# Decoder layer on one core: the gate projected together with the shared values, the shared keys by themselves, and the hand-written orders rewritten

## The reference

```
x = layernorm(x + attention(x))            # 16 query heads, 4 key/value heads of 128, rotary, softmax, Wo
x = layernorm(x + longconv(ctx, ctx, x))   # 16 heads of 8: kv = k_i v_j, causal convolution with ssm_kernel + D, times q_i
x = layernorm(x + gated(x))                # below
```

```
gating     = softmax(x @ W_gate.T)                     # 16 columns
indicator  = one_hot(argmax(gating)); top1 = max(gating)
q, k, v    = split(x @ W_qkv.T)                        # 16 heads of 16 each
k_shared   = sum over heads of indicator * k           # one key of 16 per token
v_shared   = sum over heads of indicator * top1 * v    # one value of 16 per token
att        = softmax(causal(q . k_shared / sqrt(16)))  # per head
y          = att @ v_shared
```

## Time and profile before

| | |
|---|---|
| runs | median 321.51 us of 3 (321.10 to 321.72) |
| profiled execution | 321.38 us, of it 319.6 us span |
| TensorE busy | 95% of the span |
| VectorE, ACT, GpSimd busy | 78%, 72%, 63% |
| chain that ended last | TensorE 72%, VectorE 14%, ACT 4%, GpSimd 2%, issue 6% |
| mean granted TensorE clock | 0.993 of 2.4 GHz |

### The profile page before, as it was taken

How to read it: one execution, slowest core, us unless ns; L and a number is a source line. 1 busy time by engine, 2 the same in 40 slices (tenths; PEclk the granted TensorE clock), 3 DMA queues, 4 the chain that set the end, 5 groups by cost and what they waited for, 6 DMA issues and landing times.

```text
span 319.6 us, 6276 instructions
## 1 busy us (share of the span) xinstructions
PE 305.0 (95%) x2073; PEld 242.0 (76%) x2073; DVE 250.6 (78%) x504; ACT 230.4 (72%) x695; POOL 201.2 (63%) x289
## 2 busy tenths in 40 slices
PE   6997999999999999999999999999999999999981
PEld 2896898889888889888878979877557666666550
DVE  3779868847976776776686898989999999986764
ACT  3889597869778777767875687733578877788780
POOL 0698885766754777656393278995986976720031
PEclk9999999999999999999999999999999999999997
DMA  5961103101010313213000000000000000000010
GB/s 179 295 281 49 53 3 98 30 6 67 2 33 2 114 37 104 78 37 108 0 3 0 2 1 1 2 0 3 0 3 0 18 1 3 16 3 18 17 35 33
DMA packets 6176, 13.87 MB, mean 43 GB/s; under 512 B 896, under 2 KB 3328, under 8 KB 5888
## 3 DMA queue, kind: packets, MB, share of 16 engines
q1 hardware_dynamic: 5872, 13.34, 12.7%
q10 hardware_dynamic: 272, 0.13, 0.1%
HBM read 12.42 MB, written 1.05 MB: 42 GB/s over the span
## 4 chain that ended last, share of the span: by engine, by line
PE 72%; DVE 14%; issue 6%; ACT 4%; DMA 2%; POOL 2%; SPq 0%; POOLq 0%; DVEq 0%; ACTq 0%
PE bank L415 16%; PE bank L563 14%; PE bank L452 8%; PE bank L437 7%; PE bank L524 4%; PE bank L674 3%; PE bank L632 3%; DVE t_cos L1811 3%; PE bank L685 2%; PE bank L547 2%; DMA w_raw<-in_wqkv 2%; PE bank L542 2%; DVE fneg_max L1868 2%; PE bank L544 2%; PE bank L669 1%
## 5 line engine op out<-in xcount | busy, mean ns | idle before, releaser
L2320 POOL TENSOR_TENSOR t_sin<-rot,sin 128x512 f32<-128x512 f32 x36 | 46.8, 1307 | 31.1 <-ACT rot L1151 25.4
L2348 POOL TENSOR_TENSOR prob<-prob,rden 128x512 f32<-128x512 f32 x32 | 37.2, 1164 | 33.9 <-DVE rden L1711 33.8
L1186 ACT ACTIVATE prob<-bank,neg_max 128x128 f32<-128x128 f32 x128 | 45.4, 377 | 2.3 <-DVE neg_max L1704 2.2
L563 PE MATMUL bank<-wo_hi,head_hi 128*128 128x256 f32 x128 | 40.2, 314 | 0.0
L1266 ACT ACTIVATE prob<-bank,fneg_max 128x128 f32<-128x128 f32 x128 | 36.6, 379 | 4.7 <-DVE fneg_max L1868 4.7
L415 PE MATMUL bank<-x_hi,w_hi 128*128 128x512 f32 x96 | 33.5, 429 | 3.4 <-DVE t_cos L1619 1.9
L563 PE MATMUL bank<-wo_lo,head_hi 128*128 128x256 f32 x128 | 36.0, 281 | 0.0
L563 PE MATMUL bank<-wo_hi,head_lo 128*128 128x256 f32 x128 | 35.9, 280 | 0.0
L1150 ACT COPY rot<-bank 64x512 f32<-64x512 f32 x40 | 23.4, 584 | 13.9 <-PE bank L415 12.5
L2310 POOL TENSOR_TENSOR kv<-ctxT 128x256 f32<-128x256 f32 (+3 forms) x64 | 31.8, 529 | 1.0 <-PE bank L437 1.0
L1619 DVE TENSOR_TENSOR t_cos<-bank,cos 128x512 f32<-128x512 f32 x36 | 24.6, 687 | 9.5 <-ACT rot L1151 9.0
(11 more groups left out here) (134 smaller groups left out, 807.3 us busy)
## 6 DMA issues: line engine op xcount, KB each, us to landing
w_raw<-in_wqkv SPq DMA_DIRECT2D x4, 768.0 KB, 4.4
toep<-in_toep SPq DMA_DIRECT2D x8, 256.0 KB, 2.8
wo_raw<-in_wo SPq DMA_DIRECT2D x4, 512.0 KB, 3.5
ctxT<-in_ctx SPq DMA_DIRECT2D x1, 1024.0 KB, 4.9
x<-in_x SPq DMA_DIRECT2D x1, 1024.0 KB, 9.6
out<-x SPq DMA_DIRECT2D x8, 128.0 KB, 1.7
wf<-in_wf SPq DMA_DIRECT2D x1, 784.0 KB, 4.7
x_raw<-in_xt SPq DMA_DIRECT2D x2, 256.0 KB, 4.5
```

Source lines behind the costliest of these rows:

```text
L563: last = pe.matmul(acc_bank[k // 2][:, (k % 2) * D:(k % 2 + 1) * D], hp[:, k % 2, h * P:(h + 1) * P], wp[:, g % 2, h, :], start=(h + n == ...
L1186: last = act.activation(prob[:, k % 2, h * P:(h + 1) * P], score_bank[k % 2][:, h * P:(h + 1) * P], ACT.Exp, bias=neg_max[:, k % 2, h:h + ...
L2320: pool.tensor_tensor(t_sin[:, par, :].rearrange("p (b t) -> p b t", b=BH), rot[:, par, :].rearrange("p (b t) -> p b t", b=BH), sin[:, :].u ...
L2348: pool.tensor_tensor(own, own, rden[:, k % 2, :].unsqueeze(2).to_broadcast([P, HG, P]), ALU.mult).then_inc(norm_done, 1)
```

## The change

The gate's 16 columns join the 256 of the shared values in one matmul of 272 columns (per c), into `kvf_bank`; the shared keys get a matmul of their own, 256 columns, into the upper half of `tf_bank`, beside the queries. The gate no longer waits for `kblock_done`, the keys do. `query_project` loses its wait for `gate_done`. The mask becomes two products, one from each bank, and waits for `qf_done`, the copy of the queries out of `tf_bank`. The lists of TensorE, ACT, VectorE and GpSimd are rewritten from the start to the end; SP's isn't. The functions:

```diff
-            def gate_project(b):
+            def value_project(b):
                 j = b % 2
                 pe.wait_ge(in_ffn, 48)
                 pe.wait_ge(x2copy_done, b + 1)
+                if b == 0:
+                    pe.wait_ge(acc_done, 2 * UNITS - 1)
+                at_least(pe, masked_done, b, 1)
+                at_least(pe, ynorm_done, b, 3)
+                for c in range(C):
+                    last = pe.matmul(kvf_bank[:, 0:D + FH], x2T[:, j, c * P:(c + 1) * P],
+                                     wf[:, c, 2 * D:3 * D + FH], start=(c == 0), stop=(c == C - 1))
+                last.then_inc(gate_mm_done, 1)
+
+            def key_project(b):
+                j = b % 2
                 at_least(pe, kblock_done, b, 1)
                 for c in range(C):
-                    last = pe.matmul(tf_bank[:, D:D + FH], x2T[:, j, c * P:(c + 1) * P],
-                                     wf[:, c, 3 * D:3 * D + FH], start=(c == 0), stop=(c == C - 1))
-                last.then_inc(gate_mm_done, 1)
...
+                    last = pe.matmul(tf_bank[:, D:2 * D], x2T[:, j, c * P:(c + 1) * P], wf[:, c, D:2 * D],
+                                     start=(c == 0), stop=(c == C - 1))
+                last.then_inc(kvf_done, 1)
 
             def query_project(b):
                 j = b % 2
-                pe.wait_ge(gate_done, b + 1)
...
-                act.mul(gate[:, :], tf_bank[:, D:D + FH], -1.0).then_inc(gate_done, 1)
+                act.mul(gate[:, :], kvf_bank[:, D:D + FH], -1.0).then_inc(gate_done, 1)
...
                 dve.wait_ge(kvf_done, b + 1)
-                dve.tensor_tensor(kv_masked[:, :, :, :],
-                                  kvf_bank[:, :].rearrange("p (n d h) -> p n d h", n=2, h=FH),
-                                  chosen[:, :].unsqueeze(1).unsqueeze(2).to_broadcast([P, 2, FD, FH]),
-                                  ALU.mult).then_inc(masked_done, 1)
+                dve.wait_ge(qf_done, b + 1)
+                for n, source in enumerate((tf_bank[:, D:2 * D], kvf_bank[:, 0:D])):
+                    last = dve.tensor_tensor(kv_masked[:, n, :, :], source.rearrange("p (d h) -> p d h", h=FH),
+                                             chosen[:, :].unsqueeze(1).to_broadcast([P, FD, FH]), ALU.mult)
+                last.then_inc(masked_done, 1)
```

The ramp, ACT and then VectorE:

```diff
             split_x(1)
+            split_wo(0)
             copy_v(0)
-            split_wo(0)
             exps(0, 0)
...
             exps(0, 2)
-            first_conv_copy()
             item(0, "Q1")
...
             split_x(1)
+            row_max(0, 0)
             value_low(0)
-            row_max(0, 0)
             row_max(0, 1)
...
+            cos_item(0, "K")
             row_max(0, 2)
-            cos_item(0, "K")
+            row_max(0, 3)
+            prob_low(0, 0)
             cos_item(0, "Q0")
-            prob_low(0, 0)
-            row_max(0, 3)
             add_item(0, "K")
             cos_item(0, "Q1")
```

Unit 6 and blocks 0 and 1, TensorE and then ACT:

```diff
             item(6, "Q2")
+            scores(6, 3)
             item(6, "Q3")
-            scores(6, 3)
...
             values(7, 2)
-            gate_project(0)
             x1_turn(2)
-            kv_project(0, 0)
-            kv_project(0, 1)
+            key_project(0)
+            value_project(0)
+            query_project(0)
             turn(7, 3)
-            query_project(0)
+            mix_turn(1)
             values(7, 3)
             output(7, 2)
-            mix_turn(1)
+            output(7, 3)
             key_turn(0)
-            output(7, 3)
+            x2_turn(1)
             fscores(0, 0)
...
             fvalues(0, 1)
+            key_turn(1)
             fturn(0, 2)
-            key_turn(1)
             x2_turn(2)
             fscores(1, 0)
-            gate_project(2)
-            kv_project(2, 0)
+            value_project(2)
+            key_project(2)
+            query_project(2)
             fturn(0, 3)
...
             gate_copy(0)
-            mix_query(2)
+            gate_exp(0)
+            query_copy(0)
             last_prob_copy()
-            gate_exp(0)
             head_copy(7, 3)
-            query_copy(0)
             key_copy(0)
```

GpSimd at block 2, and the tail of TensorE and VectorE:

```diff
             products(2, range(0, 4))
+            products(2, range(4, HD))
             second_power(1)
-            products(2, range(4, HD))
             first_power(1)
...
             fturn(6, 2)
+            y_turn(5)
             fvalues(6, 1)
             fvalues(6, 2)
             fturn(6, 3)
-            y_turn(5)
             fscores(7, 1)
...
             last_values(0)
+            last_values(1)
             fturn(7, 2)
-            last_values(1)
             fturn(7, 3)
...
             frow_max(7, 1)
+            y_invert(5)
+            y_scale(5)
             ffn_norm(4)
             ffn_apply(4)
-            y_invert(5)
-            y_scale(5)
             ffn_norm(5)
             frow_max(7, 2)
             frow_max(7, 3)
+            ffn_apply(5)
             y_invert(6)
             y_scale(6)
-            ffn_apply(5)
             ffn_norm(6)
             ffn_apply(6)
```

More of the change, by code:

```diff
@@ L866, in _ @@
             item(4, "Q1")
+            turn(4, 1)
             values(4, 0)
-            turn(4, 1)
             item(4, "Q2")
             item(4, "Q3")
-            scores(4, 3)
+            output(3, 3)
+            output(4, 0)
+            values(4, 1)
+            turn(4, 2)
             item(4, "C20")
-            output(3, 3)
             item(4, "C21")
-            output(4, 0)
+            scores(5, 0)
             item(4, "C22")
             item(4, "C23")
-            values(4, 1)
-            turn(4, 2)
-            scores(5, 0)
+            values(4, 2)
+            turn(4, 3)
             scores(5, 1)
@@ L940, in _ @@
             output(6, 1)
+            values(6, 3)
             x1_turn(1)
             scores(7, 2)
-            values(6, 3)
+            scores(7, 3)
+            v_turn(7)
             output(6, 2)
-            v_turn(7)
             turn(7, 0)
-            scores(7, 3)
             mix_turn(0)
@@ L952, in _ @@
             values(7, 1)
+            turn(7, 2)
             output(7, 0)
-            turn(7, 2)
             output(7, 1)
@@ L1060, in _ @@
             fturn(4, 2)
+            value_project(6)
             fvalues(4, 1)
-            gate_project(6)
+            key_project(6)
+            fturn(4, 3)
             mix_turn(7)
-            fturn(4, 3)
-            kv_project(6, 0)
+            query_project(6)
             fscores(5, 1)
@@ L1507, in _ @@
             fexps(1, 0)
+            values_in(1)
             gate_copy(2)
+            query_copy(2)
             fprob_copy(0, 3)
@@ L2014, in _ @@
             cos_item(2, "Q2")
+            row_max(2, 3)
             cos_item(2, "Q3")
@@ L2073, in _ @@
             cos_item(4, "Q1")
+            prob_low(4, 1)
             add_item(4, "Q0")
+            row_max(4, 3)
+            head_low(4, 0)
             add_item(4, "Q1")
@@ L2112, in _ @@
             cos_item(5, "Q3")
+            accumulate(4, 1)
+            prob_low(5, 2)
             head_low(5, 1)
@@ L2155, in _ @@
             head_low(6, 2)
+            prob_low(6, 3)
             accumulate(6, 0)
-            prob_low(6, 3)
-            row_max(7, 2)
             invert(7, 0)
             invert(7, 1)
+            row_max(7, 2)
             head_low(6, 3)
@@ L2192, in _ @@
             gating(1)
+            add_mix(2)
+            mix_norm(2)
             frow_max(0, 2)
-            add_mix(2)
             first_apply(4)
-            mix_norm(2)
             share(1)
             second_apply(2)
-            frow_max(0, 3)
             first_apply(5)
             first_apply(6)
+            frow_max(0, 3)
             first_apply(7)
             frow_max(1, 0)
+            mix_sum(3)
             frow_max(1, 1)
-            mix_sum(3)
             gating(2)
@@ L2220, in _ @@
             frow_max(2, 2)
-            ffn_apply(0)
+            share(3)
             frow_max(2, 3)
-            share(3)
             add_mix(4)
@@ L2231, in _ @@
             mix_sum(5)
+            ffn_norm(1)
             gating(4)
             frow_max(3, 2)
+            add_mix(5)
             frow_max(3, 3)
-            add_mix(5)
             mix_norm(5)
             share(4)
+            y_invert(2)
             second_apply(5)
-            ffn_norm(1)
+            y_scale(2)
             mix_sum(6)
             frow_max(4, 0)
-            y_invert(2)
-            y_scale(2)
             frow_max(4, 1)
+            gating(5)
             add_mix(6)
+            share(5)
+            frow_max(4, 2)
             mix_norm(6)
-            gating(5)
-            frow_max(4, 2)
             frow_max(4, 3)
             ffn_apply(1)
-            share(5)
+            second_apply(6)
             y_invert(3)
-            second_apply(6)
+            y_scale(3)
             mix_sum(7)
@@ L2256, in _ @@
             frow_max(5, 1)
-            y_scale(3)
+            ffn_norm(2)
+            gating(6)
```

(9 more changed lines are left out.)

574 lines of the change are left out of this document (273 added, 301 removed).

## The result

The changed kernel takes 324.33 us (median of 4; 323.74 to 324.40) against 321.62 for the kernel before (median of 4) beside it: a ratio of 1.0084, 95% interval 1.0071 to 1.0097. It is slower by 2.7 us, outside the range given and on the other side. The profiled execution took 323.74 us, 321.9 of them span.

A forecast was written before the change was run, and what follows sets the result against it. It saw a TensorE stall in the ramp, then TensorE and VectorE both full while mixing runs beside the gated stage, then TensorE alone. 321.4 - 0.9 - 1.3 + 0.3 - 0.6 = 318.9 us, range 316.2 to 321.8.

The forecast's parts named there:

- The ramp: Up to about 40 us: an earlier key sum on VectorE removes TensorE's stall, 1.3 us gained of 1.67.
- Rival (2): In the ramp: the key sum misses its gap and waits for GpSimd's split again, 320.2 us; chance 0.16.
- my walk: In the ramp: the key sum reaches VectorE at about 26.9, ahead of GpSimd's split; 0.4 us decide over 2.
- The matmuls and the mask: Gated blocks: 3.1 us come off TensorE's work over eight blocks; the split mask costs VectorE 0.5 us.
- What of it reaches the end: Gated blocks: 0.1 us a block for five, full 0.39 in the last; 0.9 us gained after the mask.
- rival (3): TensorE is the true bound throughout, so all of 2.6 us arrives, 317.2 us; chance 0.15.
- the new wait: VectorE's mask also waits for the queries' copy; new orders hide it, 0 us, bounds 0 and 7.
- the stages between: Between ramp and tail: one small wait goes, later copies and turns cost; net 0.3 us lost, bounds 0.8 either way.
- rival (1): Ahead of VectorE's mask: the queries' copy is late; at 0.6 us a block, 323.7 us; chance 0.12.
- those for "wrong": VectorE waits on w_raw's copy, key sum at 2 us or more, new TensorE waits at 40 to 180 over 1 us.
- those for "right": Included VectorE over 95% from 240 to 280 us and last maxima within 0.3 us of their scores.
- The tail: At the end: last maxima start about 0.9 us earlier and last_turn_copy can gain; 0.6 us gained, bounds 0 and 1.0.

The follow-up runs named there:

- e8_gate_twice: The kernel before with the new ramp alone (319.93 us), with the gate's matmuls done twice: 322.81 us.
- e9_between: Changed functions on e7_attention, key projection right ahead of the second pair of scores, queries right behind, queries' copy drawn ahead on ACT: 328.16 us.
- e6_old_in_new: The changed kernel's orders throughout with the old functions, without the mask's wait for the queries: 327.0 us.
- e7_attention: The kernel before, old functions, with the new ramp and attention orders up to about 210 us, joint mended, old gated order: 319.15 us.
- e15_together: e7_attention with gate, both halves and queries standing together on TensorE from block 1 on, where the first of them stood: 335.52 us.
- e13_scores_ahead: The kernel of e11_apply_back with the second pair of scores drawn ahead of one or both remaining projections in blocks 2 to 7: 329.13 us.
- e11_apply_back: The changed kernel with first_apply(2) at its old place on VectorE, behind prob_copy(7,2): 323.68 us.
- e1_ramp: The kernel before, old functions, with the new orders of four engines up to about 40 us alone: 319.93 us.
- e17_tail: e7_attention with the new order of the tail alone, and GpSimd's third_power(4) behind add_ffn(5): 318.71 us.
- e5_wait: The kernel before with one line more, the mask also waiting for the copy of the queries: 334.88 us.
- e3_gated: The changed functions with old orders up to about 210 us and the new orders for the gated stage alone: 327.53 us.
- e4_functions: The changed functions with new orders up to about 210 us, joint not mended, then the old gated order, adapted: 331.09 us.

## Why the prediction was wrong

**The ramp was right.** The key sum:

```profile
27.21 0.98 DVE L1621 TENSOR_TENSOR k_rope<-t_cos,t_sin 128x512 f32<-128x512 f32 x1
```

It lasts 0.98 us in place of 2.77, and 1.6 us are gained against the 1.3 forecast. Rival (2) falls. The margin was thinner than in my walk, though, and part of it luck. The maxima come 0.3 earlier and not 0.6, and the sum starts at 27.21 and not at 26.9. It is 0.37 ahead of GpSimd's split because the split starts later too, at 27.58 in place of 27.29:

```profile
27.58 2.87 POOL L2332 TENSOR_TENSOR wo_lo<-wo_raw,wo_hi 128x1024 fp32r<-128x1024 f32 x1
```

Had the split stayed where it was, 0.08 us would have been left. (Nor does such a sum last 0.6 us otherwise: the eight of the kernel before last 0.68 to 2.77 us, 0.99 in the median.)

**The matmuls and the mask were costed nearly right.** In the timeline above value_project takes 1.02 us from its start to the next and key_project 0.86, 1.88 against the 1.77 forecast; TensorE's busy time falls by 2.5 us against 3.1. (It isn't so that only four short matmuls go: there are 2073 records as before, since wide ones of 272 and 256 columns, four each, come in place of four of 512.) The two masks take 0.66 (254.77 to the reciprocal's start at 255.43) against the 0.60 of the earlier trace rows: the 0.06 of the forecast. By the Trainium skill's page "VectorE: DVE Perf Modes", section on the TRN2 errata, the split would cost 0.157 us a block, an estimate from its figure; the starts decide otherwise.

**What of it reaches the end was sized too low.** I counted 0.9 us, since VectorE at 9.67 of 10 was to set the pace for five blocks. In the old order a microsecond of TensorE's time is worth 0.8 (e8_gate_twice), in the new order the edit gains 2.7 us, in the order of e9_between 1.65. That was rival (3)'s reading. A busy share of 97% did not make VectorE the bound.

**The step that failed** is the new wait, "I take 0 for the wait, bounds 0 and 7", together with the stages between, "0.3 lost". The first half holds: 0.7 us of wait are left. But 0 was the price of the wait, not of its cover. The cover was the new gated order, above all the new place of the projections, and I named it as a reason for the 0 without asking what stands behind it now. In five of the eight blocks that is the second pair of scores: all three projections stand ahead of it, 2.77 us (249.48 to 252.25), where the gate and one half had stood, 1.30 us. The new order costs 7.9 us with the old functions (e6_old_in_new against e7_attention), where I had 0.3 lost. The steps of the runs are 321.5 - 1.6 (ramp) - 0.8 (attention) + 7.9 (gated order) - 2.7 (edit) = 324.3; they add up by themselves, as each is the difference of two kernels in the chain, and what they show is the sizes.

Which moves of the new order carry the 7.9 us is not shown. e15_together shows that the place of the projections is enough to lose more than that in the old order of the other engines, and the changed kernel's rows show late scores; but e13_scores_ahead, which undoes the late scores, was slower. The place of `first_apply(2)` is a further part, 0.7 to 1.4 us by e11_apply_back.

So rival (1) had the right conflict and the wrong place: the wait for the copy of the queries was to return on VectorE, at 323.7; it was bought off by the order, which cost more than the 4.8 us of that rival. That its time comes so near the 324.3 measured is luck, as the edit's 2.7 us were sized too low in it. The conflict comes from the bank. By the Trainium skill, "PSUM — Partial Sum Buffer", section on bank collisions, two engines may not access one bank in the same partitions at once, reads against reads included; that agrees with the wait that the code has, and no run here tried to do without the order that it makes. Before, the queries were on nobody's way to the mask; with the keys in their bank, 1.05 us of projection and 0.4 of copy are.

**The signs.** Of those for "wrong" none came: no waits for w_raw's copy in several blocks, no key sum of 2 us, no wait of TensorE from 40 to 180 us. What failed were two of those for "right". VectorE was to be over 95% from 240 to 280; it is at 8.56, 9.09 and 9.59 of 10 up to 270. And the last maxima were to start within 0.3 us of their scores; in the changed kernel they start 0.77 behind the scores' end (307.92 + 1.13, then 309.82). My list of wrong signs had no line for waits of VectorE for scores.

**The stages between 40 and 200 us** were taken as worth nothing; e7_attention against e1_ramp makes it 0.8 us. **The tail**, 0.6 in the forecast, comes out at 0.4 by e17_tail, which isn't settled.

## What to carry to other kernels

When a new wait is priced at nothing because the work that it waits for is drawn ahead, price the drawing ahead: list what that work now stands in front of, on each in-order engine. A line that adds the wait alone to the old kernel, and the old functions in the new order, separate the two in two runs; here they gave 10 to 13 us and 8 us, where the edit itself gains 2.7. Before two values that are needed at different times come to share a bank, price the order that this forces on their readers and writers against the saving, here some 0.3 us of matmul a block.

## What the runs showed of the hardware

**A scalar operation that several products hold up.** `first_apply(2)` lasts 0.44 us in the kernel before. In the changed kernel, on VectorE's and then GpSimd's timeline:

```profile
208.50 2.24 DVE L1763 TENSOR_SCALAR x<-x,mean_var,rstd 128x256 f32<-128x256 f32 x1
```

```profile
208.36 0.54 POOL L338 TENSOR_TENSOR q_rope<-y,qmix 128x160 f32<-128x160 f32 x1
...
210.49 0.47 POOL L335 TENSOR_TENSOR q_rope<-y,qmix 128x64 f32<-128x64 f32 x1
```

It starts among GpSimd's products and ends with the row of them nearly through, so it lasted through four whole products and parts of two, not one. That GpSimd held it up is read from these times; not every operation of this shape beside products is slow (0.40 us at 211.26). In e11_apply_back, with this operation out of the way, the next scalar operation lasted 1.49 us at 209.17. The Trainium skill, "SBUF — State Buffer", section "SBUF: two separate sides", speaks of a loser that blocks for the whole instruction; here it was several.

**A gap, then a lower clock.** In e5_wait, in a table of 2 us stretches:

```profile
236.00:238.00 2.00, 0.86 (x5) 0.46 (x6) 1.97 (x6) 0.48 (x2) 2.00 (x7) 1.00 0.00 0
238.00:240.00 2.00, 2.00 (x12) 1.09 (x12) 2.00 (x4) 1.70 (x6) 2.00 (x4) 0.85 0.00 0
240.00:242.00 2.00, 2.00 (x6) 1.24 (x6) 2.00 (x3) 1.21 (x5) 2.00 (x5) 0.50 0.04 12
```

TensorE had been busy 0.86 of 2 us; then the granted clock falls to 0.50, the lower level of 1.2 GHz, and stays there until 248. Two records of a half projection at 240.53 last 2.05 us against 1.02. Not every gap is followed by it: from 222 to 224 TensorE stood idle for 0.88 us, and the clock stayed at 1.00. Nor does it come alike in every execution: e5_wait's range from 331.6 us, at a mean granted clock of 0.993, to 336.3 at 0.980, and e15_together's from 331.9 (0.988) to 336.8 (0.968). So a wait that empties TensorE is paid twice at times, and the wait of e5_wait costs 10 us (331.6 against 321.4) where the clock holds. The quickest executions of e3_gated, e4_functions and e13_scores_ahead, at 0.993 to 0.995, took 326.0, 329.0 and 327.7 us, 1.4 to 2.1 below their medians. The changed kernel's profiled execution shows 1.00 in all the stretches above and a mean of 0.993, as in the kernel before; at 323.74 against 321.38 us it is still 2.4 slower, so that much of its loss is not of this kind.
